# A private zero row for each partition in the gathers of a graph kernel

## The reference

```python
x = segment_sum(w[:, None] * x[src], dst, num_segments=n)   # three hops in a row
out = out + x
```

## Time and profile before

| what | value |
|---|---|
| median of three runs | 9969.62 us (9963.71 to 10013.37) |
| the profiled execution | 10019.39 us |
| its span, first to last instruction | 10017.7 us |
| around the span | 1.7 us |
| instructions | 117,643 |

### The profile page before, as it was taken

One profiled execution on the slowest core, in us unless ns is written; L12 is line 12 of the kernel. 1 busy time (PEld: TensorE's weight loads), 2 busy tenths in 40 slices (PEclk: granted clock), 3 DMA queues, 4 the chain that ended last, 5 costly groups with the idle time before them and its releaser, 6 DMA issues. The chain is left out here.

```text
span 10017.7 us, 117643 instructions
## 1 busy us (share of the span) xinstructions
PE 6852.6 (68%) x25794; PEld 5061.9 (51%) x25794; DVE 5368.5 (54%) x21147; ACT 3631.6 (36%) x11422; POOL 6775.8 (68%) x6677
## 2 busy tenths in 40 slices
PE   7599786708879644448888068787882587989800
PEld 4355443306767533336666056666671466767600
DVE  9799898704422333336666556666667665221210
ACT  0011111104411333335555556666675565111100
POOL 7777777777657777777776066665770575767677
PEclk9899999855555555555555555555555555555555
DMA  6222211246668544433333487888886887985611
GB/s 141 56 58 47 54 21 40 66 55 148 137 82 106 102 100 96 98 83 98 97 95 83 100 112 122 108 119 112 104 107 131 128 125 106 100 91 76 72 41 39
DMA packets 1874472, 916.11 MB, mean 91 GB/s; under 512 B 1662957, under 2 KB 1700905, under 8 KB 1873861
## 3 DMA queue, kind: packets, MB, share of 16 engines
q0 software_dynamic: 213248, 215.45, 26.6%
q1 hardware_dynamic: 795544, 499.16, 18.5%
q10 hardware_dynamic: 865196, 196.73, 9.8%
HBM read 629.66 MB, written 286.87 MB: 91 GB/s over the span
## 5 line engine op out<-in xcount | busy, mean ns | idle before, releaser
L1427 POOL DMA_INDIRECT work<-table,end_idx x3136 | 3136.8, 1000 | 2012.9 <-issue 920.0
L957 PE MATMUL bank<-work 128*128 128x64 f32 x7056 | 2423.8, 448 | 1397.6 <-DMA work<-table,end_idx 1220.9
L960 PE MATMUL bank<-work 32*128 32x64 f32 x7820 | 2679.6, 444 | 342.5 <-ACT work L969 339.3
L957 PEld LDWEIGHTS bank<-work 128*128 128x128 f32 x7056 | 1765.3, 310 | 1821.0 <-issue 1416.7
L960 PEld LDWEIGHTS bank<-work 32*128 32x128 f32 x7820 | 1945.1, 308 | 816.2 <-ACT work L969 377.5
L302 ACT ACTIVATE work<-work 128x64 f32<-128x64 f32 x5488 | 2099.4, 432 | 496.1 <-DVE work L293 434.0
L969 ACT ACTIVATE work<-bank 32x64 f32<-32x64 f32 x3920 | 850.3, 217 | 2563.4 <-PE bank L960 2064.9
L269 DVE BATCH_NORM_STATS2 work<-work 128x6 f32<-128x64 f32 x5488 | 739.2, 211 | 796.1 <-ACT work L302 737.5
L1656 POOL DMA_INDIRECT acc<-nodes,work x784 | 794.5, 1013 | 287.3 <-issue 226.1
L638 POOL DMA_INDIRECT acc<-node_tab,acc x784 | 770.6, 983 | 258.7 <-issue 258.7
L899 DVE TENSOR_TENSOR work<-work,skey_col 128x896 f32<-128x896 f32 x504 | 547.8, 1087 | 241.3 <-DMA work<-skey 119.1
(11 more groups left out here) (165 smaller groups left out, 8203.1 us busy)
## 6 DMA issues: line engine op xcount, KB each, us to landing
work<-skey SPq DMA_DIRECT2D x560, 448.0 KB
table<-work ACTq DMA_DIRECT2D x336, 224.0 KB, 7.1
work<-table,end_idx POOLq DMA_INDIRECT x3136
work<-xd SPq DMA_DIRECT2D x84, 448.0 KB, 4.0
nodes<-zeros ACTq DMA_DIRECT2D x8, 3136.0 KB, 35.8
work<-lowrow SPq DMA_DIRECT2D x196, 128.0 KB, 3.0
work<-in_x SPq DMA_DIRECT2D x56, 448.0 KB, 4.0
nodes<-work ACTq DMA_DIRECT2D x56, 448.0 KB, 3.8
```

The source lines that it names most:

```text
L957: ins = nc.tensor.matmul(o, sel[:, k, :], rows[:, k, :], start=True, stop=not before)
L960: ins = nc.tensor.matmul(o, self.join[b % 2][:, k, :], self.inn[(b + k + 1) % 2], start=False, stop=True)
L1427: nc.gpsimd.indirect_dma_start(got[b][:, k, :], None, source, bass.IndirectOffsetOnAxis(ap=idx[:, t:t + 1], axis=0)).then_inc(got_in[b].se ...
```

## The change

Each partition gets a zero row of its own. A column `zero_row` holds `ZROW + p` and `-1 - ZROW - p` for partition p, and `assemble` takes these two columns in place of the two constants. The rows of zeros were there already.

```diff
+        zero_row = sb("zero_row", [P, 2])
...
-                    nc.vector.tensor_copy(lane_col[:], lane)
+                    nc.vector.tensor_copy(lane_col[:], lane).then_inc(s_low, 1)
+                    dve.wait_ge(s_low, 1)
+                    nc.vector.tensor_scalar(zero_row[:, 0:1], lane_col[:, 0:1], 1.0, float(ZROW), ALU.mult, ALU.add)
+                    nc.vector.tensor_scalar(zero_row[:, 1:2], lane_col[:, 0:1], -1.0, -1.0 - ZROW, ALU.mult, ALU.add)
                     dve.wait_ge(s_in, 32)
...
-                    dve.wait_ge(s_low, 1)
+                    dve.wait_ge(s_low, 2)
...
-                        c.do(nc.vector.scalar_tensor_tensor(rec[:, :, 3], obase, -1.0 - ZROW, odeg, ALU.add, ALU.add))
+                        c.do(nc.vector.scalar_tensor_tensor(rec[:, :, 3], obase, zero_row[:, 1:2], odeg, ALU.add, ALU.add))
...
-                        c.do(nc.vector.tensor_scalar(rec[:, :, 3], rec[:, :, 3], float(ZROW), None, ALU.add))
+                        c.do(nc.vector.tensor_scalar(rec[:, :, 3], rec[:, :, 3], zero_row[:, 0:1], None, ALU.add))
```

## The result

The changed kernel's median is 9,869.9 us (9,868.1 to 9,874.8, four runs). The kernel before, beside it, has 9,991.5 us (9,963.7 to 10,014.0, four runs, three of them those from which the prediction started). The ratio is 0.988 with a 95% interval of [0.985, 0.991]: 1.2% faster, 122 us against the runs beside it and 100 against the median that the prediction started from.

A forecast was written before the change was run, and what follows sets the result against it. It took POOL as the floor of most hops, with DVE's load waits above it in three dense hops, from gathers jamming the DMA engines. 146 + 27 + 19 = 192 us off 10,019 gives 9,827, rounded to 9,820; range 9,740 to 9,945.

The forecast's parts named there:

- about 0.1: Gathers' queue q0 in the hops: its share of the DMA engines falls from 0.5 to 0.64 to about 0.1.
- Nothing happens: Rival: the one row isn't the cause, or neighbouring rows jam alike; time stays at 9,970 us; chance 0.12.
- slower: Rival: 128 rows must each be found where one was open; six hops lose about 60 us each, 10,330; chance 0.03.
- Dense hops at 5782, 6394 and 7837: DVE's waits for loads there: 80.6 us gained at line 1497 and 65 at line 899, together 146 us.
- the 545 to 560 of the signs: Sign of being right: the dense hops come out at 545 to 560 us.
- most waits come back elsewhere: Rival: DVE freed from loads waits for ACT or PE; half of 192 us gives 9,923; chance 0.15.
- Dense hop at 7012: Hop of 562.3 us that stores no table: gains 27 us, down to POOL's floor of 535.
- Hop at 8435.9: Hop of 536.1 us bound by POOL: gains 19 us, down to a floor of 517.
- First hop: Hop at 2812, POOL-bound or held by the preparation of the next list: nothing counted.
- unchanged within 5: Sign of being right: the hop of 1,013 us and the last hop stay within 5 us.
- the forecast's own range: Whole kernel: 9,755 to 9,885 us, as line 899's waits are kept whole or given back whole; forecast's chance 0.58.
- the landing time of keyrank's loads: Sign of being right: keyrank's load lands in 5 to 7 us.

The follow-up runs named there:

- the a = 1 run: Changed kernel with the zero-row change only for the six hops with a = 1, the a = 0 hops reading one zero row: 9,886.3 us, 0.995 of before.
- the early loads: Kernel before, one zero row, node loads issued two groups ahead: 9,996.5 us, 0.999 of before; the same edit on the changed kernel: 9,857.7 us, 0.985.
- the first experiment: Changed kernel with the same column operations, but one zero-row address in every partition: 9,934.0 us, 1.002 of the kernel before.

## Why the prediction was right, and where its sizes were off

- **Mechanism: shown.** One address read by most of a gather's reads jams the DMA engines. One row in the new form brings the time back, all reads to one row add 16%, two rows cure it. q0's share came out at 0.10 to 0.15 in the eight hops, for "about 0.1", and the DMA share under 0.5. "Nothing happens" and "slower" are out. The Trainium skill's page "DMA: Bandwidth & Descriptors", section "Bandwidth", calls transfers under 64 KB dominated by their descriptors; the "nothing" that the prediction drew from this is not what the traces show, since gathers of one size held the engines for 2.7, 13.9 and 22.4 us.
- **Dense hops at 5782, 6394 and 7837: 114.3 us for 146, the term that was mis-sized.** The waits of the sum fell almost as forecast: line 1497's in these hops from 101.9 to 20.3 us, by 81.6 for 80.6, and line 899's by 54.4 for 65. But the hops came out at 560 to 566 us, not near 552 nor within the 545 to 560 of the signs. What was put at nothing is the wait that comes back: the prediction says that DVE's chain with ACT is late next, and gives it no price. At line 899 the keys and the loop's turn gave 95.1 us, and the wait for ACT's copy took 41.0 of them back. At line 294 the wait for ACT's square root grew by 19.6 us, and that, with smaller lines that nearly cancel, makes 136 us of freed waits into the 114 by which the hops fell. That is the rival "most waits come back elsewhere", for 32 of 146 us.
- **Dense hop at 7012: 15.1 us for 27.** The forecast took POOL's 401.9 us as fixed, but they grew to 415.7. These 13.8 us cover the 12 that are missing.
- **Hop at 8435.9: 26.2 us for 19;** at 509.9 us it went below the floor of 517 worked out for it, since POOL's gathers fell from 386.1 to 377.8 us.
- **First hop: 16.3 us where nothing was counted.** It isn't held by POOL's own work alone: line 1431's wait for ACT at line 973 fell from 31.3 to 16.5 us, and the a = 1 run shows the gain to be that of its own gathers.
- **Hop of 1,013 and last hop: +6.6 and +7.2 us** for "unchanged within 5"; **the stage behind them: +9.4 (525.6 to 535.0),** of which the prediction says nothing. POOL's transfers got longer by 6.6, 8.8 and 9.7 us. In the last hop the cause is the meeting with DVE's selects; for the other two it isn't shown.
- **Sum and median.** 151 us of the span for 192. Luck has a part in this: the stages named above fell short by 67 us together, and gains beyond those counted, in the first hop and at 8435.9, made up for 24 of these. The time of 9,870 us is 50 above the forecast of 9,820, 41 of it from the sum and 7 from the rounding, near the upper end of the forecast's own range. The prediction carried the whole sum over to the runs' median; 100 us came there, 122 and 146 against the runs beside it. The changed kernel's time was the same in both comparisons, and that of the kernel before was not, so what the change is worth depends on how dear the one row is in the lot it is set against.
- **Not readable:** the landing time of keyrank's loads, forecast at 5 to 7 us, for which the trace of after gives none.

## What to carry to other kernels

Where a gather has a default row, spread the default over several addresses: here two were enough, and the few small operations that it takes cost no time that can be seen. Look for it by engine time per gather in the DMA view, beside a gather of the same size elsewhere, not by bytes. Where the DMA engines are jammed, a wait row names the load that came last, and moving that load can hand the wait to the next, as the early loads did here; remove the jam instead. Give a price to the waits that come back (here DVE's for ACT), and take the floor of the engine behind (here POOL) with its own contention in it.

## What the runs showed that was not expected

- 128 reads of one row of 256 bytes cost some 13.8 ns each on the path (an estimate from a hop of 712.5 us), and reads of two rows by turns are nearly as cheap as of 128 (q0 14.3% against 12.8).
- With one zero row, a gather held the engines for 13.9 us in the hop at 8435.9 of before, and for 9.0 in the same hop of the first experiment, in another lot.
- A select of 1.09 us on DVE lengthened the gather on POOL that met it, in the two meetings shown by 0.37 and 0.84 us. In the last hop this was 25.0 us of 526.4; cut into seven column compares of 0.30 us, it went (946 ns per gather), and with early loads the kernel took 0.987 [0.985, 0.988] of the time before, on a chip where the kernel before took 9,941.
